# A mixture-of-experts stage whose experts each take their first 64 rows as a unit of its own, with the tokens as stationary operand in both column halves of TensorE

## What is computed

```python
probs = softmax(flat @ router_w.T)                    # 1024 tokens, 8 experts
topv, topi = top_k(probs, 2)
g = einsum('td,eid->tei', flat, w1)                   # d = 256, i = 704
u = einsum('td,eid->tei', flat, w3)
yexp = einsum('tei,edi->ted', silu(g) * u, w2)
moe_out = einsum('ted,te->td', yexp, gate_w)
```

## Time and profile before

| | us |
|---|---|
| median of 3 runs | 639.96 (639.33 to 641.6) |
| the profiled execution's own time | 641.04 |
| its span, from first to last instruction | 639.3 |
| PE busy in the span | 592.2 |
| DVE, ACT, POOL busy in the span | 460.7, 387.9, 293.8 |
| the expert stage, first gate product to the end of the last down product | 263.93 to about 449.7 |

### The profile page before, as it was taken

How to read it: one execution, slowest core, us unless ns; L and a number is a source line. 1 busy time by engine, 2 the same in 40 slices (tenths; PEclk the granted TensorE clock), 3 DMA queues, 4 the chain that set the end, 5 groups by cost and what they waited for, 6 DMA issues and landing times.

```text
span 639.3 us, 11082 instructions
## 1 busy us (share of the span) xinstructions
PE 592.2 (93%) x3725; PEld 466.4 (73%) x3725; DVE 460.7 (72%) x770; ACT 387.9 (61%) x876; POOL 293.8 (46%) x232
## 2 busy tenths in 40 slices
PE   4999779988999999999999999999999999999774
PEld 2653679988898888798889889899855555655442
DVE  6989989999999956534435442642575698999985
ACT  4589899999999956532223231311546665768543
POOL 6023599999999992222231333152113233133301
PEclk9999799999999999999999999999999999999998
DMA  8001552212121108424413441411520000000001
GB/s 283 2 1 36 159 222 63 55 52 65 50 59 58 34 7 331 138 111 173 162 52 149 158 172 41 165 34 33 172 108 1 2 1 0 1 2 1 1 0 66
DMA packets 18193, 51.44 MB, mean 80 GB/s; under 512 B 3779, under 2 KB 9540, under 8 KB 16485
## 3 DMA queue, kind: packets, MB, share of 16 engines
q1 hardware_dynamic: 15172, 41.43, 18.7%
q0 software_dynamic: 2688, 7.34, 4.0%
q10 hardware_dynamic: 288, 2.10, 0.9%
HBM read 45.95 MB, written 4.92 MB: 80 GB/s over the span
## 4 chain that ended last, share of the span: by engine, by line
PE 67%; ACT 13%; DVE 9%; issue 5%; DMA 3%; POOL 1%; POOLq 0%; DVEq 0%; ACTq 0%
PE ps L2067 13%; PE ps L2140 8%; PE ps L2075 7%; ACT arena L653 7%; PE ps L2129 4%; PE ps L2161 3%; ACT arena L668 3%; DMA moe_out<-arena,result_now 3%; PE ps L1884 3%; PE ps L1869 3%; PE ps L1966 2%; PE ps L1915 2%; PE ps L1710 2%; PE ps L2090 2%; PE ps L1719 2%
## 5 line engine op out<-in xcount | busy, mean ns | idle before, releaser
L442 POOL TENSOR_TENSOR arena<-arena 128x1024 f32<-128x1024 f32 x64 | 149.5, 2381 | 4.1 <-DVE arena L1262 3.8
L1262 DVE TENSOR_TENSOR_SCAN arena<-arena,ps 128x1024 f32<-128x1024 f32 x64 | 143.5, 2278 | 4.7 <-ACT arena L653 1.4
L2067 PEld LDWEIGHTS ps<-arena 128*128 128x128 f32 x924 | 106.1, 192 | 5.2 <-issue 4.1
L2067 PE MATMUL ps<-arena 128*128 128x128 f32 x924 | 107.4, 276 | 0.9 <-DVE arena L1360 0.3
L839 ACT ACTIVATE arena<-ps 128x256 f32<-128x256 f32 x63 | 24.1, 383 | 107.3 <-PE ps L2067 107.3
L653 ACT ACTIVATE arena<-arena,a_neg 128x510 f32<-128x510 f32 x128 | 84.6, 710 | 1.9 <-DVE arena L1262 1.7
L1869 PE MATMUL ps<-ident,arena 128*128 128x128 f32 x384 | 65.0, 279 | 9.9 <-ACT arena L664 9.0
L1884 PE MATMUL ps<-ident,arena 128*128 128x128 f32 x512 | 67.0, 273 | 2.2 <-DVE arena L1271 1.8
L668 ACT ACTIVATE arena<-arena,b_tok 128x512 f32<-128x512 f32 x96 | 64.9, 710 | 0.0
L1884 PEld LDWEIGHTS ps<-ident,arena 128*128 128x128 f32 x512 | 57.9, 141 | 3.3 <-DVE arena L1271 1.3
L2140 PE MATMUL ps<-arena 128*128 128x512 f32 x128 | 58.2, 595 | 0.0
(11 more groups left out here) (296 smaller groups left out, 1069.0 us busy)
## 6 DMA issues: line engine op xcount, KB each, us to landing
arena<-in_w_moe SPq DMA_DIRECT2D x8, 2176.0 KB, 9.3
arena<-c_dram SPq DMA_DIRECT2D x32, 256.0 KB, 3.2
arena<-in_w_o ACTq DMA_DIRECT2D x1, 2048.0 KB, 14.3
arena<-in_w_qT SPq DMA_DIRECT2D x1, 2048.0 KB, 10.3
arena<-moe_out SPq DMA_DIRECT2D x8, 256.0 KB, 5.1
arena<-in_w_q SPq DMA_DIRECT2D x1, 2048.0 KB, 10.5
x<-in_x SPq DMA_DIRECT2D x2, 512.0 KB, 4.4
arena<-in_w_in SPq DMA_DIRECT2D x2, 512.0 KB, 5.7
```

The lines of the kernel that those rows point to most:

```text
L442: pool.tensor_tensor(in_chunks(hC[unit % 3]), in_chunks(h[unit % 3]), c_bc[:, m % C_BUFS, :].unsqueeze(1).to_broadcast([P, 2, HALF]), ALU. ...
L1262: nc.vector.tensor_tensor_scan(h[unit % 3], dA[:, k, :], ps[:, 2 * k:2 * k + 2, :].rearrange("p a b -> p (a b)"), 0.0, ALU.mult, ALU.add). ...
L2067: ins = nc.tensor.matmul(ps[:, bank, c * P:(c + 1) * P], w13[:, k, chunk * P:(chunk + 1) * P], xT[:, k, :], start=(k == 0), stop=(k == KD ...
```

## The change

- Every expert now begins with a unit of up to 64 rows (`TAIL`), followed by max(1, ceil((rows - 64)/128)) full tiles. For the given inputs these are 2, 1, 2, 2, 2, 3, 1 and 2, in all 15, and 8 units of 64. The full tiles' loop runs from `first + 1`, and its body is as before.
- In a unit of 64 the tokens are the stationary operand (`xT[:, k, 0:64]`) and the weights move, up to 384 columns at a time. Two halves of the 1408 gate and up columns go to partitions 0 to 63 and 64 to 127 of banks 0 and 1, in turn: 384 and 384 columns in bank 0, 256 and 384 in bank 1, each for two depths. One Silu over 384 columns, three multiplications on DVE (`gate_tail`), three transposes to bring the channels onto partitions, two copies by ACT into `hid`, then six down products of 256 columns with 64 stationary columns, in the two column halves in turn, and a copy and an addition on DVE (`sum_tail`) that joins the halves.
- The border work of PE, ACT and DVE is placed inside the unit of 64: on PE some behind gate and up (VW steps, fp8 transposes, the keys of the last quarter) and some behind the transposes (VW steps, keys, transposed keys). DVE does `normalise_keys`, `sum_squares` and the parts of `QUANT_AHEAD` before `gate_tail`, the rest behind it. POOL's `rstd_of_keys` comes after the unit of 64. The wait for the copies before the loop is gone, but for one in expert 0.
- The places are counted in another way: one more DVE operation on 128 x 64 elements that nothing waits on at once (`behind`), one more that the next one waits for, and COLS grows from 26 to 34, so the three operations on `at_tile` have 544 elements instead of 416.
- `take_keys` is one key bank at a time, its squares a function of their own, and `ym_done` and `ymT_psum` are renamed.

```diff
 REST = FF - WHOLE * P
 W13 = 2 * FF
 MOE_W = KD * W13 + FCH * D
-OUT_TILES = 2 * TILES + E - 1
+TAIL = P // 2
+FULL_MOST = 2 * TILES + E - 1
+OUT_TILES = FULL_MOST + E
+FF_A = FCH // 2 * P
...
 norm_cols = lambda v, g, half: v[:, (g + 1) * TILES + half * HALF_TILES:(g + 1) * TILES + (half + 1) * HALF_TILES]
-VW_STEPS = {0: 6, 1: 4, 2: 4, 3: 2}
+VW_AHEAD = 6
+VW_TURNS = {0: ((6,), (7,)), 1: ((8, 9), (10,)), 2: ((11, 12), (13, 14)), 3: ((15,), ())}
 FP8_TURNS = {4: 2, 5: 0, 7: 1}
 SIZE_TURNS = {1: 2, 3: 0, 5: 1}
-QUANT_TURNS = {0: ((2, (1, 2)),), 1: ((2, (4, 5)),), 2: ((0, (1, 2)),), 3: ((1, (1,)), (0, (4, 5))), 4: ((1, (2,)),), 6: ((1, (4, 5)),)}
+QUANT_AHEAD = {1: (2, (4,)), 2: (0, (1,)), 3: (1, (1,))}
+QUANT_BEHIND = {0: (2, (1, 2)), 1: (2, (5,)), 2: (0, (2,)), 3: (0, (4, 5)), 4: (1, (2,)), 6: (1, (4, 5))}
 K_AT, KT_AT, QK_AT = 3 * PAIRS, 4 * PAIRS, 5 * PAIRS
...
     for e in range(E):
+        move_rows(last, TAIL)
         if e in NORM_TURNS:
             rstd_of_keys(NORM_TURNS[e])
-        first, last = last, pool.value_load(bounds[0:1, e + 1:e + 2], min_val=1, max_val=OUT_TILES)
-        with pool.Fori(first, last) as j:
-            move_rows(j)
+        first, last = last, pool.value_load(bounds[0:1, e + 1:e + 2], min_val=2, max_val=OUT_TILES)
+        with pool.Fori(first + 1, last) as j:
...
+    def silu_of_tail(first):
+        act.wait_ge(s["gu_psum"], first * (FCH // 2) + 1)
+        act.wait_ge(s["hid_done"], first * (FCH // 2) + FCH // 2)
+        nc.scalar.activation(act_g3[:, :, 0:P], ps[:, 0, 0:FF_A].rearrange("p (a b) -> p a b", b=P), ACT.Silu).then_inc(s["gate_act"], FCH // 2)
+
+    def take_tail_transposed(e, first):
+        act.wait_ge(s["y_psum"], first + 1)
+        for bank, cs in enumerate((slice(0, 2), slice(2, 3))):
+            act.wait_ge(s["gatedT_psum"], 2 * CI + 2 * e + bank + 1)
+            nc.scalar.activation(hid[:, cs, :], ps[:, bank, 0:(cs.stop - cs.start) * P].rearrange("p (a b) -> p a b", b=P),
+                                 ACT.Identity).then_inc(s["hid_done"], cs.stop - cs.start)
+
+    for n in range(VW_AHEAD):
+        take_values_times_output(n, (4, 5, 2, 3, 4, 5)[n])
+    act.wait_ge(s["routed"], 1)
     last = 0
     for e in range(E):
         if e in SIZE_TURNS:
             sizes(SIZE_TURNS[e])
-        for n in range(VW_STEPS.get(e, 0)):
-            take_values_times_output(step, (4, 5, 2, 3, 4, 5)[n] if e == 0 else 2 + n)
-            step += 1
-        if e in K_TURNS:
-            take_keys(K_TURNS[e], (2, 3) if e in KT_TURNS else (4, 5))
+        silu_of_tail(last)
+        if e in VW_TURNS:
+            for k, n in enumerate(VW_TURNS[e][0]):
+                take_values_times_output(n, 2 + k)
+        if e == 6:
+            take_keys(3, 0)
+            take_keys(3, 1)
+        take_tail_transposed(e, last)
+        if e in VW_TURNS:
+            for k, n in enumerate(VW_TURNS[e][1]):
+                take_values_times_output(n, 4 + k)
+        if e in (3, 4, 5):
+            take_keys(K_TURNS[e], 0)
+            take_keys(K_TURNS[e], 1)
         if e in KT_TURNS:
             take_transposed_keys(KT_TURNS[e], (4, 5))
-        if e == 0:
-            act.wait_ge(s["routed"], 1)
-        first, last = last, act.value_load(bounds[0:1, e + 1:e + 2], min_val=1, max_val=OUT_TILES)
-        with act.Fori(first, last) as j:
+        if e in K_TURNS:
+            square_keys(K_TURNS[e])
+        first, last = last, act.value_load(bounds[0:1, e + 1:e + 2], min_val=2, max_val=OUT_TILES)
+        with act.Fori(first + 1, last) as j:
             for q in range(FCH // 2):
...
-    link(nc.vector.tensor_scalar(count_i[:, :], ps[:, 0, 0:E], float(P - 1), None, ALU.add))
+    link(nc.vector.tensor_scalar(count_i[:, :], ps[:, 0, 0:E], float(P - TAIL - 1), None, ALU.add))
     link(nc.vector.tensor_scalar(count_i[:, :], count_i[:, :], 7, None, ALU.logical_shift_right))
-    link(nc.vector.tensor_scalar(count[:, 0, :], count_i[:, :], 1.0, float(P), ALU.max, ALU.mult))
+    link(nc.vector.tensor_scalar(count[:, 0, :], count_i[:, :], 1.0, 1.0, ALU.max, ALU.add))
     link(nc.vector.tensor_tensor_scan(count[:, 1, :], ones[:, 0:E], count[:, 0, :], 0.0, ALU.mult, ALU.add))
     link(nc.vector.tensor_tensor(count[:, 2, :], count[:, 1, :], count[:, 0, :], ALU.subtract))
     dve.wait_ge(s["route_psum"], 2)
-    link(nc.vector.tensor_tensor(place[:, :, :], ps[:, 1, E:E + TILES * E].rearrange("p (e i) -> p i e", e=E),
-                                 count[:, 2, :].unsqueeze(1).to_broadcast([P, TILES, E]), ALU.add))
+    rank = ps[:, 1, E:E + TILES * E].rearrange("p (e i) -> p i e", e=E)
+    nc.vector.tensor_scalar(behind[:, :, :], rank, TAIL - 0.5, float(P - TAIL), ALU.is_gt, ALU.mult)
+    link(nc.vector.scalar_tensor_tensor(place[:, :, :], count[:, 2, :].unsqueeze(1).to_broadcast([P, TILES, E]), float(P), rank, ALU.mult, ALU.add))
+    link(nc.vector.tensor_tensor(place[:, :, :], place[:, :, :], behind[:, :, :], ALU.add))
     link(nc.vector.tensor_tensor(picked[:, :, :, :], picked[:, :, :, :], place[:, :, :].unsqueeze(1).to_broadcast([P, 2, TILES, E]), ALU.mult))
     link(nc.vector.tensor_reduce(slot_f[:, 0, :], picked[:, :, :, :].rearrange("p k i e -> p (k i) e"), axis=AX.X, op=ALU.add))
     link(nc.vector.tensor_copy(slot[:, :], slot_f[:, 0, :]))
...
         of_heads = k_rs[:, :].rearrange("p (j h) -> p j h", j=2)[:, :, 4 * q:4 * q + 4]
         nc.vector.tensor_tensor(heads, heads, of_heads.unsqueeze(3).to_broadcast([P, 2, 4, DH]), ALU.mult).then_inc(s["k_normed"], 1)
+    def gate_tail(e, first):
+        dve.wait_ge(s["gate_act"], first * (FCH // 2) + FCH // 2)
+        dve.wait_ge(s["gu_psum"], first * (FCH // 2) + FCH // 2)
+        nc.vector.tensor_tensor(act_g3[:, 0:2, P:2 * P], act_g3[:, 0:2, 0:P], ps[:, 1, 0:2 * P].rearrange("p (a b) -> p a b", b=P),
+                                ALU.mult)
+        nc.vector.tensor_tensor(act_g3[0:TAIL, 2, P:2 * P], act_g3[0:TAIL, 2, 0:P], ps[0:TAIL, 1, 2 * P:3 * P], ALU.mult)
+        nc.vector.tensor_tensor(act_g3[TAIL:P, 2, P:P + REST], act_g3[TAIL:P, 2, 0:REST], ps[TAIL:P, 0, FF - FF_A:FF_A],
+                                ALU.mult).then_inc(s["gated_done"], 1)
+
+    def sum_tail(first):
+        dve.wait_ge(s["y_psum"], first + 2)
+        dve.wait_ge(s["y_free"], first + 1)
+        link(nc.vector.tensor_copy(y_row[0:TAIL, :], ps[0:TAIL, 6, 0:D]))
+        nc.vector.tensor_tensor(y_row[0:TAIL, :], y_row[0:TAIL, :], ps[TAIL:P, 6, 0:D], ALU.add).then_inc(s["y_ready"], 1)
...
     link(nc.vector.tensor_tensor(prob[:, :, :], prob[:, :, :], stat_of(2), ALU.mult))
     last = 0
     for e in range(E):
-        if e in FP8_TURNS:
-            take_fp8(sorted(FP8_TURNS).index(e), FP8_TURNS[e])
         if e - 1 in NORM_TURNS:
             normalise_keys(NORM_TURNS[e - 1])
         if e in NORM_TURNS:
             sum_squares(NORM_TURNS[e])
-        for m, parts in QUANT_TURNS.get(e, ()):
-            quantise(m, parts)
-        first, last = last, dve.value_load(bounds[0:1, e + 1:e + 2], min_val=1, max_val=OUT_TILES)
-        with dve.Fori(first, last) as j:
+        if e in QUANT_AHEAD:
+            quantise(*QUANT_AHEAD[e])
+        gate_tail(e, last)
+        if e in FP8_TURNS:
+            take_fp8(sorted(FP8_TURNS).index(e), FP8_TURNS[e])
+        take_transposed(last + 1)
+        if e in QUANT_BEHIND:
+            quantise(*QUANT_BEHIND[e])
+        sum_tail(last)
+        first, last = last, dve.value_load(bounds[0:1, e + 1:e + 2], min_val=2, max_val=OUT_TILES)
+        with dve.Fori(first + 1, last) as j:
             for q in range(FCH // 2):
                 dve.wait_ge(s["gate_act"], j * (FCH // 2) + q + 1)
...
         pe.wait_ge(s["kv_out"], (3, 4, 7, 8)[n])
         values_times_output(n, (4, 5, 2, 3)[n])
     transpose_rows(0)
-    for n in range(4, VW_STEPS[0]):
+    for n in range(4, VW_AHEAD):
         pe.wait_ge(s["kv_out"], PAIRS + n - 3)
         values_times_output(n, n)
-    step = VW_STEPS[0]
+    def tail_gate_and_up(first, w13):
+        pe.wait_ge(s["xT_done"], first + 2)
+        pe.wait_ge(s["hid_done"], first * (FCH // 2) + FCH // 2)
+        for bank, parts in ((0, ((0, 0, FF_A), (TAIL, FF_A, 2 * FF_A))), (1, ((TAIL, 3 * FF_A, W13), (0, 2 * FF_A, 3 * FF_A)))):
+            for k in range(KD):
+                for rows, at, end in parts:
+                    ins = nc.tensor.matmul(ps[rows:rows + TAIL, bank, 0:end - at], xT[:, k, 0:TAIL], w13[:, k, at:end],
+                                           start=(k == 0), stop=(k == KD - 1), skip_group_check=True)
+            ins.then_inc(s["gu_psum"], 1 + bank)
+
+    def transpose_tail(e):
+        pe.wait_ge(s["gated_done"], TILES + e + 1)
+        for bank, cs in enumerate((range(2), range(2, 3))):
+            for c in cs:
+                ins = nc.tensor.transpose(ps[:, bank, (c - cs[0]) * P:(c - cs[0] + 1) * P], act_g3[:, c, P:2 * P], ident[:, :])
+            ins.then_inc(s["gatedT_psum"], 1)
+
+    def tail_down(first, w2):
```

(76 more changed lines are left out.)

16 lines of the change are left out of this document (9 added, 7 removed).

## The result

The changed kernel takes 645.49 us (median of 6 runs, 643.39 to 646.77) beside 640.85 for the kernel before: a ratio of 1.0069, 95% interval 1.0046 to 1.0091. It is slower by 4.6 us, where 633.5 was forecast. How the two figures go together is told with that experiment.

A forecast was written before the change was run, and what follows sets the result against it. PE's products were taken to bound the kernel. Stage 115.8 + 38.6 + (23.6 - 1.3) + 0.5 + 1.2 = 178.4 against 185.7 us, -7.3, plus 0.8 routing: 639.96 becomes 633.5 us, range 630 to 640.5 (own case 630 to 637).

The forecast's parts named there:

- What bounds the stage, six tiles saved, 7.72 us each: Expert stage: PE's products set its time; six of 21 full tiles go, leaving 15 x 7.72 = 115.8 us.
- Gate and up, 8 x 0.34 = 2.7: Unit of 64, gate and up: eight record pairs at 0.34 us each take 2.7 us, bounds 2.6 and 4.75.
- second case: Units of 64: each product group pays one record alone at its begin, 4.5 us in all, time 638.0; 13%.
- the fifth: Units of 64: column halves do not overlap with 384 columns, 26 us more, time 660; 3%.
- Down, "6 x 0.225 = 1.35": Unit of 64, down: six record pairs at 0.225 us take 1.35 us, up to 2.6 without overlap.
- a small price: Units of 64 on PE: draining at tiling changes costs 0.11 us per return to whole width, 0.22 a unit.
- The other queues ... Both cost nothing, with little room for the gather: Expert stage: POOL's row gathers (5 us against units of 6.5 to 7.5) and weight loads (9.2 against 15) add nothing.
- third case: Row supply: gathers come after PE's row transposes, 4 to 7 us in all, time 637.5 to 640.5; 10%.
- Hand-overs: Units of 64: PE's waits for its own results through DVE and ACT, 1.2 us exposed in experts 4, 5, 7.
- the slower case: Units of 64: PE waits 1.15 + 0.64 us each because DVE or ACT come late, time 646.7; 9%.
- Routing, 0.8: Routing ahead of the stage: extra and longer DVE operations add 0.8 us on the path, bounds 0.4 and 1.2.
- The sum: Whole kernel: stage 7.3 us less and routing 0.8 more give -6.5, median 639.96 to 633.5; 63%.

The follow-up runs named there:

- that experiment: The changed kernel again, no edit, twelve more runs on one chip beside the kernel before: 643.38 us, ratio 1.0016 (0.9998 to 1.0035).
- the gather first: Changed kernel with POOL issuing the next gather before it waits for the previous scatter: 639.36 us, ratio 0.9978 to the kernel before.
- both edits: Changed kernel with all 128 rows in the sixth down product and POOL's next gather before the scatter wait: 635.81 us, in more runs 633.99.

## Why the prediction was wrong

- **What bounds the stage, six tiles saved, 7.72 us each**: right. The 15 full tiles ran at 7.7, 7.8 behind column halves. The earlier trace rows leave out one wait of 0.3 us of PE for DVE (L1360, `take_fp8`, at 426.40), so the waits of before were 1.0 us and not 0.7.
- **Gate and up, 8 x 0.34 = 2.7**: right, 2.73. The second case, in which each group pays a record alone, did not come, nor did the fifth.
- **Down, "6 x 0.225 = 1.35"**: wrong. The sum counts 0.11 more for the return to the whole width, so 1.46 was forecast to the next group; 2.01 came, and 1.45 without the change of form. For eight units that is 4.4 us of stage by the runs (182.1 with the gather first alone, 177.7 with both edits). The step took its price from a row in which all products have the form 128*64, while the code of the change gives the sixth product 64 rows. The Trainium skill's sentence on draining at a change of the tiling mode ("TensorEngine Tiling (Array Packing)", Key Properties) was put aside as "a small price" because only the changes between groups were counted, and the one inside a pair was overlooked. There it costs 0.56 us by the runs, so the trace agrees with the rule.
- **"The other queues ... Both cost nothing, with little room for the gather"**: wrong, 4.8 us of stage. POOL's time was read at 283.81 and 285.99, inside an expert. At a border the weights' load makes the scatter land 5 us later, and the trace of before had that. The prediction charged the load only with its own deadline (9.2 us against 15), and not with what it holds up. Its third case had the symptom and the price (4 to 7 us, 10%), put down to `rstd_of_keys` and short experts. These are not the main cause: the wait is longest in expert 3, which has no `rstd_of_keys` and two full tiles, and with the load left out or the gather first, `rstd_of_keys` as it was, no wait is left. They have a part in one of the five: the wait of 0.8 us in expert 7, where POOL's 1.7 us of `rstd_of_keys` (426.26) stood between expert 6's late scatter and the gather at 429.02.
- **Hand-overs**: 1.2 us in experts 4, 5 and 7 were forecast; it was 0.4 in expert 0, which was not in the list, and in four later profiles about 0.2 in expert 7. The border work covers the rest, and the slower case built on them is refuted. DVE's late parts, which were to stay hidden, cost 0.2 to 0.4 us in expert 3 in three profiles with a shorter down.
- **Routing, 0.8**: 0.7.
- **The sum.** With both failed steps mended, the stage is 177.7 and 178.2 us where 178.4 was worked out, and the time 634.0 to 635.8 where 633.5 was forecast. The other terms held to about a microsecond together, in part because small misses cancel (0.8 too much for the hand-overs, 0.3 too little for the waits). The two that failed are 9.2 us of stage together and turned the sign.

## What to carry to other kernels

Here a wait for a small transfer lasted as long as the large one issued just before it. So look at the rows at a border, where both are issued, not inside a loop, and let no request that the bottleneck needs stand behind such a wait. When two column halves are to share TensorE's time, give both products of a pair the same number of rows, with zeros if need be. A repair that shows little alone may be hidden behind another wait: try the two together before dropping one.

## What was not expected of the hardware

- A change between the forms 128*64 and 64*64 inside a pair took the pairing away and cost 0.56 us (2.01 against 1.45), ahead of a pair 0.14.
- A scatter of 128 rows issued 0.8 us behind a 2176 KB load let POOL go on 7.9 us after its issue, 3.4 with the load left out or issued after it. A gather issued 5.6 us after the load was not late for PE 6.9 us later.
